# An order of their own for the last seven slots of a two-layer graph attention kernel

## What is computed

```python
h = jnp.maximum(_layernorm(x, axis=-1), 0.0)
x = x + _L0_gnn_ref(h, adj, ...)   # m = h@map_w.T; cos of m's heads; q, k from m; softmax(q k) * (cos > 0.1);
                                   # 8 heads; times values; relu(AxW / denom)
h = jnp.maximum(_layernorm(x, axis=-1), 0.0)
x = x + _L1_gnn_ref(h, adj, ...)   # q, k, v = h@Wq, h@Wk, h@Wv; 4 heads; masked softmax; @ Wo + bo
```

## Time and profile before

| | |
|---|---|
| median of 3 runs | 2671.84 us (2670.15 to 2672.61) |
| the profiled execution's own time | 2665.52 us |
| its span in the profile | 2663.7 us |
| PE, POOL, DVE, ACT busy, share of the span | 96%, 81%, 77%, 64% |
| mean granted TensorE clock | 0.981 |
| first matmul of slot 126 | 2578.10 us |
| from there to the end of the span | 85.6 us |

### The profile page before, as it was taken

The page is one execution under the profiler, slowest core; times in us unless marked ns, Lnnn a source line. Parts: engine busy times, 40 slices in busy tenths (PEclk is TensorE's granted clock), DMA queues, the critical chain, the costliest instruction groups (busy, mean ns, idle before and its releaser), DMA issues.

```text
span 2663.7 us, 78789 instructions
## 1 busy us (share of the span) xinstructions
PE 2566.1 (96%) x30681; PEld 2064.2 (77%) x30681; DVE 2060.3 (77%) x3456; ACT 1710.0 (64%) x4501; POOL 2168.1 (81%) x2449
## 2 busy tenths in 40 slices
PE   5789999999999999999999999999999999999995
PEld 3577888787788878878888887887888788788773
DVE  4267878878887888888788878888888878888873
ACT  1257667666766766766676676667667666766762
POOL 0368888888888888888888888888888888888873
PEclk7899999999999999999999999999999999999997
DMA  3145666556556656655665565566556556565643
GB/s 108 37 81 106 113 118 131 109 117 119 115 112 119 126 113 110 127 109 115 123 121 113 116 126 110 114 123 119 115 116 127 108 116 121 121 112 119 119 91 75
DMA packets 829123, 299.07 MB, mean 112 GB/s; under 512 B 772560, under 2 KB 778192, under 8 KB 828752
## 3 DMA queue, kind: packets, MB, share of 16 engines
q1 hardware_dynamic: 828752, 294.04, 56.4%
HBM read 75.80 MB, written 33.55 MB: 41 GB/s over the span
## 4 chain that ended last, share of the span: by engine, by line
PE 89%; POOL 3%; DVE 3%; ACT 2%; DMA 2%; issue 1%; SPq 1%; DVEq 0%; ACTq 0%; POOLq 0%
PE unit_ps L1265 47%; PE unit_ps L1273 24%; PE s_ps L1283 4%; PE s_ps L1323 3%; PE c_ps L1283 3%; PE unit_ps L1342 2%; PE unit_ps L1357 2%; PE unit_ps L1283 2%; PE unit_ps L1333 1%; POOL inv_norm L625 1%; DMA o_t<-o_hl 1%; ACT e_ec L708 1%; DVE qk_hl L943 1%; POOL inv_rows L631 1%; PE unit_ps L1234 1%
## 5 line engine op out<-in xcount | busy, mean ns | idle before, releaser
L708 ACT ACTIVATE e_ec<-e_ec,neg_mx 128x128 f32<-128x128 f32 x1024 | 397.9, 391 | 4.2
L1265 PE MATMUL unit_ps<-h_t,w_m_hi 128*128 128x256 f16 x2048 | 342.2, 274 | 9.5 <-DMA h_t<-h_hl 9.5
L1265 PE MATMUL unit_ps<-h_t,w_k_hi 128*128 128x256 f16 x2048 | 344.4, 273 | 0.0
L1265 PE MATMUL unit_ps<-h_t,w_q_hi 128*128 128x256 f16 x2048 | 342.8, 273 | 0.0
L1273 PE MATMUL unit_ps<-w_v_hi,h_t 128*128 128x512 f16 x1024 | 324.9, 379 | 0.0
L576 POOL TENSOR_TENSOR e_ec<-e_ec 128x1024 f16<-128x1024 f32 x128 | 287.6, 2247 | 15.7 <-ACT e_ec L735 15.7
L1265 PE MATMUL unit_ps<-h_t,w_m_lo 128*128 128x256 f16 x1024 | 280.4, 274 | 0.0
L1265 PE MATMUL unit_ps<-h_t,w_k_lo 128*128 128x256 f16 x1024 | 280.1, 274 | 0.0
L1265 PE MATMUL unit_ps<-h_t,w_q_lo 128*128 128x256 f16 x1024 | 279.1, 273 | 0.0
L943 DVE TENSOR_TENSOR qk_hl<-qk_sb,qk_hl 128x512 f16<-128x512 f32 x128 | 164.7, 1287 | 117.7 <-ACT qk_hl L797 117.6
L1265 PEld LDWEIGHTS unit_ps<-h_t,w_m_hi 128*128 128x128 f16 x2048 | 196.1, 98 | 39.0 <-issue 9.9
(11 more groups left out here) (175 smaller groups left out, 7722.7 us busy)
## 6 DMA issues: line engine op xcount, KB each, us to landing
xa<-in_x_dram SPq DMA_DIRECT2D x128, 256.0 KB, 3.4
xres<-in_x_dram SPq DMA_DIRECT2D x128, 256.0 KB, 2.8
out_dram<-ybuf SPq DMA_DIRECT2D x128, 256.0 KB, 2.5
h_t<-h_hl SPq DMA_TRANSPOSE x256, 3.2
ec_t<-e_ec SPq DMA_TRANSPOSE x256, 3.2
adj_in<-in_adj_dram SPq DMA_DIRECT2D x128, 16.0 KB, 2.0
p_t<-p_hl SPq DMA_TRANSPOSE x128, 3.3
o_t<-o_hl SPq DMA_TRANSPOSE x128, 3.8
```

Of the source, the lines that this page charges most:

```text
L708: ins = nc.scalar.activation(e[:, h, :], e[:, h, :], ACT.Exp, bias=neg[:, h:h + 1], scale=SCALE, accum_out=sums[:, h:h + 1])
L1265: ins = nc.tensor.matmul(out, w[a][:, i, c * P:(c + 1) * P], h[:, :, b, i, :], start=n == 0, stop=n == len(passes) - 1)
```

## The change

The slots 126 to 132 leave `over_slots` and get, on every engine, a list written out step by step; the slots before them keep their lists and their waits. With it come an own order of PSUM units (`LATE_UNITS`), own buffers for the scores, the f16 parts and the turned parts of the last graph [127] (they lie in `m_sb`, `sq_t` and `sq_rest`, which are out of use by then), a semaphore `et_last` for its turn, one semaphore `y_out` per output buffer, and `result_base` for one slot at a time. In the tail `e_lower` runs on DVE instead of POOL.

```diff
+LATE = 2
+LATE_UNITS = (
+    (-2, "s1a"), (-2, "s1b"), (-2, "wo"), (-2, "lv"), (-1, "lq"), (-1, "lk"), (0, "lv"), (-1, "o1e"), (0, "s1a"), (0, "s1b"),
+    (-1, "o1o"), (1, "lq"), (1, "lk"), (-1, "wo"), (2, "s1a"), (2, "s1b"), (1, "o1e"), (1, "o1o"), (0, "wo"), (2, "lv"),
+    (1, "wo"), (3, "o1e"), (2, "wo"), (3, "o1o"), (3, "wo"), (4, "wo"),
+)
+        e_last = m_sb[:, :, :].rearrange("p c n -> p (c n)").rearrange("p (h n) -> p h n", h=H)
...
-                    wait(sp, av_full, s.at(lambda t: t))
+                    wait(sp, av_full, s.at(lambda t: t if t != B - 1 else t - 1))
...
+            a, b, c, d, e, f, g = late_slots(B)        # SP
+            turn_o1(a)
+            turn_h1(a)
+            load_residual(a)
+            turn_e(a, 0, e_hi)
+            turn_e(a, 1, e_lo)
+            turn_h1(b)
+            store(a)
+            load_residual(b)
+            turn_e(b, 0, e_hi)
+            turn_e(b, 1, e_lo)
+            turn_p1(a, 4)
+            turn_p1(a, 3)
+            turn_h1(c)
+            turn_h1(d)
+            turn_o1(b)
+            turn_p1(c, 4)
+            turn_p1(c, 3)
+            turn_o1(c)
+            store(b)
+            turn_p1(e, 4)
+            turn_o1(d)
+            store(c)
+            turn_p1(e, 3)
+            turn_o1(e)
+            store(d)
+            turn_o1(f)
+            store(e)
+            turn_o1(g)
+            store(f)
+            store(g)
...
+            h1_lower(a)                                # POOL
+            v_lower(a)
+            norm_l1(a)
+            h1_lower(b)
+            keep_and_block(a)
+            result_base(a)
+            result_base(b)
+            keep_and_block(b)
+            p1_lower(a, 4)
+            p1_lower(a, 3)
+            norm_l1(b)
+            h1_lower(c)
+            norm_l1(c)
+            h1_lower(d)
+            o1_lower(b, 5)
+            result_base(c)
+            p1_lower(c, 4)
+            o1_lower(b, 4)
+            p1_lower(c, 3)
+            p1_lower(e, 4)
...
+            scores_exp(a)                              # ACT
+            h1_rows(a)
+            h1_upper(a)
+            e_upper(a)
+            lv_upper(a)
+            scores_exp(b)
+            e_upper(b)
+            l1_exp(a, 4)
+            l1_exp(a, 3)
+            lqk_upper(b, "lq", lq_hl, LQ)
+            lqk_upper(b, "lk", lk_hl, LK)
+            h1_rows(b)
+            h1_upper(b)
+            lv_upper(c)
+            h1_rows(c)
+            h1_upper(c)
...
+            scores_mask(a)                             # DVE
+            attended(a)
+            x1_stats(a)
+            scores_mask(b)
+            gate(a)
+            l1_mask(a, 4)
+            l1_max(a, 4)
+            e_lower(a)
+            l1_mask(a, 3)
+            l1_max(a, 3)
+            result(a)
+            lv_lower(a)
+            gate(b)
+            e_lower(b)
+            attended(b)
+            x1_stats(b)
+            attended(c)
+            x1_stats(c)
+            lqk_lower(b, "lq", lq_hl, LQ, 0)
...
+            l1_mask(e, 3)
+            l1_max(e, 3)
+            result(b)
+            o1_rows(d, 5)
+            result(c)
+            o1_rows(d, 4)
+            lv_lower(e)
+            result(d)
+            o1_rows(f, 5)
+            result(e)
+            o1_rows(f, 4)
+            result(f)
+            result(g)
...
-                    if not s.odd and s.has(-4):
-                        u = s.unit("s1b")
-                        pe.wait_ge(unit_out[u.bank], u.before + 1)
...
+            scores(a)                                  # PE
+            cosines(a)
+            l1_scores(a)
+            weighted_sums(a)
+            output(a)
+            scores(b)
+            l1_values(a)
+            cosines(b)
+            weighted_sums(b)
+            lqk_part(b, "lq", w_lq)
+            lqk_part(b, "lk", w_lk)
+            weighted_sums(c)
+            l1_values(c)
+            l1_sums(b, 5)
+            l1_scores(c)
+            l1_sums(b, 4)
+            lqk_part(d, "lq", w_lq)
+            lqk_part(d, "lk", w_lk)
+            output(b)
+            l1_scores(e)
+            l1_sums(d, 5)
+            l1_sums(d, 4)
+            output(c)
+            l1_values(e)
+            output(d)
+            l1_sums(f, 5)
+            output(e)
+            l1_sums(f, 4)
+            output(f)
+            output(g)
```

More of the change, by code:

```diff
@@ L68, with __init__, place_units @@
 BANKS = 4
-class Unit:
-    def __init__(self, bank, before, full):
-        self.bank, self.before, self.full = bank, before, full
+LATE = 2
+LATE_UNITS = (
[3 rows of a table added]
+)
+class Unit:
+    def __init__(self, bank, before, full, last):
+        self.bank, self.before, self.full, self.last = bank, before, full, last
+def place_units(graphs):
+    order = [(u, what, 0 <= u + ahead < graphs) for u in range(FIRST_SLOT, graphs - LATE) for what, ahead in UNITS[u % 2]]
+    order += [(graphs + u, what, True) for u, what in LATE_UNITS]
+    units, used, last, full = {}, [0] * BANKS, [None] * BANKS, 0
+    for place, (u, what, there) in enumerate(order):
+        bank = place % BANKS
+        units[u, what] = Unit(bank, used[bank], full + 1, last[bank])
+        if there:
+            used[bank] += 1
+            full += 1
+            last[bank] = (u, what)
+    return units
 class Slot:
+    units = {}
     def __init__(self, n, i, graphs):
         self.n, self.i, self.graphs = n, i, graphs
+        self.late = n >= graphs - LATE
         self.odd = n % 2
@@ L100, in unit @@
     def unit(self, name, back=0):
[L102 to L112, removed]
+        return self.units[self.n - back, name]
 FIRST_SLOT = -6
@@ L733, in e_upper @@
                     act.wait_ge(ec_done, s.at(lambda t: t + 1))
[L734 to L735 removed]
+                    if not s.late or s.n == B - 2:
+                        wait(act, et_in, s.at(lambda t: 32 * t))
+                    nc.scalar.activation(e_hl_of(s)[:, 0], e_of(s)[:, :, :], ACT.Copy).then_inc(e_hi, 1)
             def v_upper(s, name, ahead):
@@ L749, in lv_upper @@
                     act.wait_ge(unit_full, u.full)
-                    if s.has(-5):
-                        act.wait_ge(unit_full, s.unit("o1o", back=1).full)
+                    if s.has(-7):
+                        act.wait_ge(unit_full, s.unit("o1o", back=3).full)
                     r = (s.n - 4) % 4
@@ L1255, in start_unit @@
                 wait(pe, unit_out[u.bank], u.before)
+                if u.last and u.last[1] == "s1a":
+                    both = s.units[u.last[0], "s1b"]
+                    pe.wait_ge(unit_out[both.bank], both.before + 1)
                 return unit_ps[:, u.bank]
```

102 lines of the change are left out of this document (80 added, 22 removed).

## The result

The changed kernel takes 2654.16 us, the median of 6 runs (2649.89 to 2660.38), beside 2670.99 us for 6 runs of the kernel before in the same set (2664.76 to 2674.53; three of the six are those that the prediction started from): a ratio of 0.9943, 95% interval [0.9925, 0.9961]. In the first set of experiments it took 2654.04 (6 runs), beside 2667.41 for 17 runs of the kernel before: 0.9951 [0.9937, 0.9965]. So it is faster by 17 and 13 us in the medians; the predicted time of 2662.5 is 8.3 too high and the range (from 2657.5) misses it by 3.3.

The account below looks back on a forecast made before the run. PE bounds the body, but from 2578.10 us the tail is a chain of latencies through every engine. Gain 12.2 up to l1_scores(e), less 2.8 behind it: 2671.84 - 9.35 = 2662.5 us, range 2657.5 to 2668.0.

Parts of the forecast that it names:

- the last line of the sum: From span to run median: the runs' median lay 6.3 above the profiled execution, carried over; 2671.84 - 9.35 = 2662.5 us.
- e of 126: Slot a: `e_lower` on DVE waits for POOL's first base, 2.1 (bounds 1.2 and 3.4); lqk(b) starts 2.5 earlier.
- The length of lqk(b): Layer-1 lq and lk matmuls of slot b on PE, no bank wait between them: 7.5, between 5.6 and 10.6 by clock.
- From lqk(b) to l1_scores(e): Tail from 2596.5 to 2623.65, through x1 and h1 of graph 127 and lqk(d); l1_scores(e) 12.2 earlier than before.
- From there to the end: Behind l1_scores(e): six outputs in a row tied by one o_t, 30.7 against 27.9, giving back 2.8 of the gain.
- PE keeps its clock: Rival: shorter gaps leave PE at 1.00 in outputs, lqk(d) and lqk(b); 8.7 more gain, 2653.8; chance 0.13, wholly or partly.
- the own e buffers: Last graph's own buffers: covered by lqk(b) on PE, all but some 0.7 us of their gain; costed at nothing.
- no effect: Rival: the chain was bound by the layer-1 pair's latency anyway, leaving 2671.8; chance 0.02.
- slower: Rival: five landings of the turned o1 at 5.7 each through the single buffer, 2679.0; chance 0.04.
- the one that ends at 2668: Rival: o1 landings of 3.3 and a second base ahead of `e_lower` cut the gain to 3.8; chance 0.15.
- Until 2578.10 I expect no difference: Body ahead of the tail: units, banks and waits of the older slots stay the same, so no change in time.
- the kept clock halfway: Lower end of the range: half of the gain from PE staying at its high clock, put at 2657.5 us.

Follow-up runs that it names:

- result_early: Changed kernel with `result(b)` ahead of the l1 masks and maxima of e on DVE; 2654.85 us, ratio to the kernel before 0.9945.
- after_again: The changed kernel run once more, unaltered; 2654.04 us, ratio to the kernel before 0.9951.
- old_tail: Changed kernel with the last seven slots back on old lists, unit order, buffers and `e_lower` on POOL; 2665.54 us, ratio to the kernel before 0.9994.
- two_o: Changed kernel with two buffers each for o1's f16 parts and the turned o1 from graph 123 on; 2651.23 us, ratio to the kernel before 0.9937.
- k_first: Changed kernel with ACT's upper copy of k's first half ahead of `o1_upper(s, 4)` in the body's odd slots; 2664.44 us, ratio to before 0.9986.
- attended_late: Changed kernel with `attended(a)` and `x1_stats(a)` back behind gate, l1 masks and maxima on DVE, POOL and ACT orders adapted; 2659.05 us, ratio 0.9963.
- no_races_two_o: Changed kernel with scores(b) ahead of output(a) on PE, both `result_base` steps moved on POOL, two o1 buffers from graph 123; 2647.44 us, ratio 0.9924.

## Why the prediction was off

- **The step that failed first is the last line of the sum**: "the median of the runs lies 6.3 above that. I carry the difference over". That median was of 3 runs. 47 runs of the kernel before, over four sets and with these three among them, have a median of 2667.55 (2660.97 to 2674.53): the three stood 4.3 above it. Of the 8.3 by which the forecast was too high, 4.3 are this base. With it mended, the same ledger gives 2658.2. Measured against the six runs of its own set alone (2670.99) it would be 0.85 for the base and 7.5 for the gain; the changed kernel's two sets agree (2654.16 and 2654.04), so I go by the 47.
- **The other 4.0 are the size of the gain**: 9.35 forecast, 13.4 in the medians (2667.41 to 2654.04). Of it 2.27 is found in the tail of the profile of after (76.25 against 73.98), in two mis-sized terms of about the same size, ahead of lqk(b) and behind l1_scores(e):
  - *e of 126.* "I take the wait for the first base alone: 2.1" was 1.22, the lower bound, as DVE got in 0.07 ahead of POOL; in result_early it was 2.17, as forecast. The rule of the Trainium skill ("SBUF — State Buffer", in its section on the two sides), that one waits for a whole instruction of the other, fits both. Which one was left open by the lists. Then lqk(b) stood behind the turned e (landed at 15.84) and the weighted sums of 126, 1.50 at the low clock, which the ledger had left out; it had the turned h1 there, which landed 0.3 before lqk(b) began. 1.2 earlier in sum. The length of lqk(b), 7.49, was forecast as 7.5.
  - *From lqk(b) to l1_scores(e)* 27.22 against 27.15: right in sum, so l1_scores(e) comes 1.13 earlier by what was won ahead of it.
  - *From there to the end* 29.56 against 30.7. The landings were right (2.41, 2.42, 2.42 for 2.45), the stall too; the outputs were 2.19, 2.75 and 1.95, where I took 2.76 for each: the clock stood at 1.00 for a part of them. In after_again they took 1.48, 1.74 and 2.76, and the part 28.65. That is the rival "PE keeps its clock", partly come true, with 0.13 of the chance; it gave 1.4 here. Its price of 1.45 for an output was a little high: 2.76 less 1.48 is 1.28.
- **What remains**, 1.8 of the 4.0, is within what single profiles differ by: after_again has a tail of 72.94, and old_tail, whose tail is that of before, one of 87.36 for 85.6. The means of the two pairs, 86.5 and 73.5, differ by 13.0, about what the medians do. So the ledger's start, one profile's 85.6, was itself a sample of one.
- **Right**: where the gain comes from, and its order of size at each milestone; no effect of the own e buffers that can be told; part of the gain given back in the output chain, through the one buffer o_t (two_o shows what it costs); no landing of o_t over 3 there. For that I had named a reason that is not so, that SP has nothing else in flight in the tail: a store was issued 0.43 before the last turn of before, and in after one follows each of the last turns by 1.25. The landings of 2.4 came with them. The rivals of no effect and of slower are refuted by the ratio, and the one that ends at 2668 by the landings.
- **"Until 2578.10 I expect no difference"** is right for the mean (old_tail 0.9994) and false for one execution: slot 126 starts between 2571.12 and 2584.62 in profiles of kernels with this body (k_first aside). I read single profiles as if they were good to 1 us before the tail. The late pairs explain a part: 10 instead of 5 at 1.5 each is 7.5, for 6.5 of difference. They do not explain all: attended_late has 3 and starts 7.0 before the kernel with 5. The first row maximum on DVE, ahead of all pairs, shows where more of it lies: at 136.1 in before, 137.1 in after, 133.2 in attended_late, and up to 138.4 (no_races_two_o). From there to the row maximum of slot 126 it is 2444.2, 2449.7 and 2440.1. So of the 6.5 of after 1.0 is there before the first pair, and of the 7.0 of attended_late 2.9. What moves the start was not tried and stays open.
- **The range** was made of costs in the tail alone. A term for the base, with three runs that lie within 2.5 us while 47 lie within 13.6, would have let it reach down to the result. Its lower end was also added up wrong: the kept clock halfway is 2662.5 less half of 8.7, 2658.15, not 2657.5.

## What to carry to other kernels

Once the matrix engine has no more long work, write each engine's list by the chain of latencies: what starts the next landing goes first (here x1 of the last graphs), and whatever ties a landing to the work before it (the one o_t) gets a second buffer there. Where two engines reach a shared resource within a few tenths of a us, let the order of the lists decide it, or count both outcomes. And carry a forecast from one profile to a median only with more than three runs of it: here 47 executions of one program, in four sets, lay up to 13.6 us apart.

## What was not expected of the hardware

- Both outcomes of one meeting of DVE and POOL cost POOL the same: its two additions took 3.49 and 3.48, beside 2.50 in the earlier trace rows with DVE out of the way. In after it is the first addition that took 2.27 instead of 1.27; in result_early DVE's subtraction was long (2.17) and then the second addition, 2.26. DVE ahead is cheaper by 0.95 for DVE and not dearer for POOL. The shortest, middle and longest of POOL's two additions in ns, of after and of result_early:

```profile
L629 POOL TENSOR_TENSOR ybuf<-x,bias_o x2: 1257/1764/2271, 2595.9 to 2598.2; 128x512 f32<-128x512 f32 x2
```

```profile
L629 POOL TENSOR_TENSOR ybuf<-x,bias_o x2: 1264/1760/2256, 2590.7 to 2591.9; 128x512 f32<-128x512 f32 x2
```

- The turn of o1, the same transfer each time, landed after 2.41 to 2.44 in the last links of after, with at most a store beside it, after 4.13 in slot a of result_early, and after 5.4 in the late pair above (issued at 2486.17, ACT released at 2491.62).
- Gaps of 1.3 to 1.9 on PE left the clock at 1.00 throughout (two_o), and one of 2.46 did too (result_early, first matmul behind it 0.39), while one of 2.38 was followed by 0.61 in the same profile. In after a gap of 1.88 was followed by 0.61 and one of 2.54 by 0.39. So the length of a gap alone did not tell what clock the output behind it got.

```profile
2648.12 0.61 PE L1460 MATMUL unit_ps<-w_o_hi,o_t 128*128 128x512 f16 x1 [1.88 <-DMA o_t<-o_hl]
```
